# Moving the weights' scaling behind Z, and splitting the first sum rows, in a two-layer graph network on one core

## The chip, the cores and the metric

The kernel runs on one core of a Trainium2 chip. The metric is the device time of one execution in microseconds (us). Three runs of the kernel before took 913.83, 913.29 and 912.90 us; the median is 913.29.

## The reference, cut to what matters

x is 4096 x 256, adj a 4096 x 4096 matrix of zeros and ones. Two layers, each followed by a residual sum and a layer norm:

```python
# layer 0
deg = maximum((adj != 0).sum(-1), 1)
a_norm = rsqrt(deg) * (adj + I) * rsqrt(deg)     # one degree for rows and columns of a row: 1/deg
x = layernorm(x + relu((a_norm @ x + x) @ W0 + b0))
# layer 1
attn_a = sigmoid(concat(adj @ x, x) @ Wa.T + ba);  attn_b likewise with Wb, bb
h = x @ W_sa;  scores = (h @ a_left)[:, None] + (h @ a_right)[None, :]
e = where(adj != 0, exp(-leaky_relu(scores, 0.01)), 0)
x_a = e / (sum(e, 1) + 1e-5) @ h
x_b = adj @ (x @ W_gcnb) + b_gcnb
x = layernorm(x + sigmoid(attn_a * x_a + attn_b * x_b))
```

(`node_degree` comes in as a column, so both factors of a_norm belong to the row.)

## The kernel before, in words

The 4096 rows are 32 tiles of 128 (T=32). Everything is ordered by hand: each engine runs its own list of instructions in program order, and semaphores (`S[...]`) tie them together. There is no planner.

**Stage 1, Z.** Z = x @ W0. For each tile t, TensorE transposes x (`xt_step`, L1277), ScalarE copies the transpose out (`xt_copy`, L521), TensorE multiplies by W0 (`z_step`, L1288) into one of two banks (so `z_step(t)` waits until Z of t-2 is copied out), and ScalarE (first ten tiles) or VectorE copies Z out (`z_copy`, L526 and L810). Z is then split into a high fp16 part on ScalarE (`y_hi`, L533) and a low part on VectorE (`y_lo`, L837). In steady state the split of tile t-2 follows the copy of tile t; after the loop come the splits of tiles 30 and 31.

**The adjacency** arrives as 128 strips of 512 KB through a ring of six (RING). SP, the queue of the transfers, issues strip s after strip s-6 is cast (L334). Even strips are cast to one-byte codes by ScalarE (L513), odd ones by VectorE (L797). A quarter is 16 strips, and holds the codes for four row tiles; all codes of a quarter are also written to memory (L322), behind the issue of the strip six after its last.

**Stage 2, sums.** For each row tile n, `sum_rows` (L1305) adds adj rows times Z: two matmuls (high, low) for each of the 32 row blocks jb, into the bank of n. Rows 0 to 15 of tiles 0 to 3 are done during stage 1 (`pass0_rows`). Their rows 16 to 31 (OUTER=16) come after a wait for all 32 low parts (`ylo_ready`). When a tile is complete (`acc_done`), VectorE does `degree`, `residual`, `stats` (together `head(n)`, L950 to L978), GpSimd the power and the shift (L436, L439), ScalarE `normalize` (L549, gives `x1_ready`). TensorE transposes x1 (`t_step`, L1325; `t_step(0)` stands between tiles 2 and 3), ScalarE and VectorE split it (`x1t_copy` L558, `x1t_lo` L940), and `p_step` (L1340) multiplies it by the scaled weights `wps`. `proj_copies` on ScalarE and `h_lo`, `forms_lo` on VectorE turn this into operands of the later stages; `p_step(n)` also waits for `h_lo(n-1)`. From tile 4 on, a tile's t_step and p_step stand between quarters of its sum matmuls.

**The weights.** `weight_norm` (L859 to L861) ends with a maximum; GpSimd takes a power of it (L420); `weight_scale` (L866 to L876) waits for that (`alpha_pow`) and works out the scale and its relatives; `weight_parts` (L882, L884) write the high and low part of the weights, `wps`.

**Later stages** compute the adj products of layer 1 from seven products for each panel, and the attention with its exponentials, in a loop over 16 panels, with waits only on earlier work.

Of the kernel before, what the change touches and what calls it, by code (L numbers as in the profile page):

```python
# [17 lines left out]
T = N // P  # L18
# [4 lines left out]
PT = 4  # L23
# [5 lines left out]
ZACT = 10  # L29
ZLAG = 12  # L30
OUTER = 16
WTS = 13
WTS_AT = 8
WARM = 20
# [53 lines left out]
def build(nc, x, adj, W0, b0, Wsa, asa, Wg, bg, Wa, ba, Wb, bb, out):  # L88
# [121 lines left out]
    with ExitStack() as ctx:  # L210
        ps = ctx.enter_context(nc.psum_tensor("ps", [P, 8, 512], F32))
        block_sem = lambda name: ctx.enter_context(nc.semaphore(name))
        S = {}
# [60 lines left out]
        def h_place(n):  # L274

            return hst[:, n % 2] if n < T - 2 else fb[:, n]
# [129 lines left out]
        def _(pool):  # L406
# [14 lines left out]

            pool.wait_ge(S["wts_in"], 16 * (WTS - 1))

# [59 lines left out]
        def cast_waits(eng, s):  # L483

            qq = s // GS
            eng.wait_ge(strip_in[s % RING], 16 * (s // RING + 1))
            if qq >= SLOTS:
                eng.wait_ge(S["acc_done"], PT * (qq - SLOTS + 1))
                eng.wait_ge(codes_out[qq % SLOTS], 32 * (qq // SLOTS))

        def codes_of(s):
            return codes[:, s // GS % SLOTS, :, s % GS * SJ:(s % GS + 1) * SJ, :].rearrange("p h j i -> p j h i")
# [3 lines left out]
        def split_at(t):  # L496

            upto = lambda i: 0 if i < ZACT else min(i - 1, 2 * (i - ZACT) + 2)
            return range(upto(t - 1), T if t == T else upto(t))
# [285 lines left out]
        def _(dve):  # L785
# [7 lines left out]
            def cast(count):  # L793

                for s in [next(todo) for _ in range(count)]:
                    cast_waits(dve, s)
                    dve.tensor_scalar(codes_of(s), strip_of(s), float(EDGE - NONE), float(NONE),  # L797
                                      ALU.mult, ALU.add).then_inc(S["cast_dve"], 1)
# [8 lines left out]
            def z_copy(t):  # L807

                dve.wait_ge(S["z_done"], t + 1)
                dve.tensor_copy(zf[:, t, 0:D], ZP(t)).then_inc(S["zf_dve"], 1)  # L810
# [23 lines left out]
            def y_lo(t):  # L834

                dve.wait_ge(S["yhi_ready"], t + 1)
                dve.scalar_tensor_tensor(out=y[:, t, 1, 0:D], in0=zf[:, t, 0:D], scalar=sc[:, SX],  # L837
                                         in1=y[:, t, 0, 0:D], op0=ALU.mult, op1=ALU.subtract
                                         ).then_inc(S["ylo_ready"], 1)

            def weight_column(k, c):

                dve.wait_ge(S["wts_in"], 16 * (WTS - 1))
                st.then(dve.scalar_tensor_tensor(out=wsum[:, 0:D], in0=wp[:, k, WG:WC], scalar=1.0,
                                                 in1=asab[:, c * D:(c + 1) * D], op0=ALU.mult, op1=ALU.mult,
                                                 accum_out=wp[:, k, GC + 2 + c:GC + 3 + c]))
                st.sync()

            def weight_squares():

                flat = lambda a: a.rearrange("p k c -> p (k c)")
                st.then(dve.tensor_tensor(flat(wsq[:]), flat(wp[:]), flat(wp[:]), ALU.mult))
                st.sync()
                dve.tensor_tensor(wsq[:, 1, :], wsq[:, 0, :], wsq[:, 1, :], ALU.add).then_inc(S["wsq_ready"], 1)

            def weight_norm():

                dve.wait_ge(S["wsum_ready"], 1)
                st.then(dve.tensor_reduce(sc[:, TMP], wsum[:], AX, ALU.max))  # L859
                st.sync()  # L860
                dve.tensor_scalar(sc[:, WMX], sc[:, TMP], 1e-30, None, ALU.max).then_inc(S["wnorm_ready"], 1)  # L861

            def weight_scale():

                dve.wait_ge(S["alpha_pow"], 1)
                st.then(dve.tensor_scalar(sc[:, AL], sc[:, WN], F16_TOP / D ** 0.5, None, ALU.mult))  # L866
                st.sync()
                st.then(dve.reciprocal(sc[:, IAL], sc[:, AL]))
                st.sync()
                st.then(dve.tensor_scalar(sc[:, HINVA], sc[:, IAL], 1.0 / EDGE_VAL, None, ALU.mult))  # L870
                st.then(dve.tensor_scalar(bgb[:], bgb[:], sc[:, AL], 0.5 * EDGE_VAL, ALU.mult, ALU.mult))
                dve.memset(hst[:, :, :, HC:ROW], 0.0)
                st.then(dve.tensor_scalar(sc[:, EXS], sc[:, IAL], 1.0 / PROJ, None, ALU.mult))
                st.then(dve.tensor_scalar(sc[:, QSC], sc[:, IAL], -SLOPE / PROJ, None, ALU.mult))
                st.then(dve.tensor_scalar(sc[:, WS], sc[:, AL], D ** 0.5, None, ALU.mult))
                dve.tensor_scalar(sc[:, QB], sc[:, IAL], -SLOPE * F16_TOP, None, ALU.mult).then_inc(S["alpha_ready"], 1)  # L876

            def weight_parts(part):

                st.sync()  # L880
                if part == 0:
                    st.then(dve.tensor_scalar(wps[:, :, 0, :], wp[:], sc[:, WS], None, ALU.mult))  # L882
                else:
                    dve.scalar_tensor_tensor(out=wps[:, :, 1, :], in0=wp[:], scalar=sc[:, WS], in1=wps[:, :, 0, :],  # L884
                                             op0=ALU.mult, op1=ALU.subtract).then_inc(S["wps_ready"], 1)
# [7 lines left out]
            for t in range(ZACT, T):  # L893
                z_copy(t)
                for i in split_at(t):
                    y_lo(i)
                if 10 <= t < 26 and t % 2 == 0:
                    cast(1)
                if 18 <= t < 22:
                    weight_column((t - 18) // 2, t % 2)  # L900
                if t == 22:
                    weight_squares()
                if t == 26:
                    weight_norm()
                if t == 28:
                    weight_scale()
                if t in (29, 30):
                    weight_parts(t - 29)
            for t in split_at(T):
                y_lo(t)  # L910

# [10 lines left out]
            def h_lo(n):  # L922
                t, h = n, h_place(n)
                dve.wait_ge(S["hhi_ready"], n + 1)
                dve.scalar_tensor_tensor(out=h[:, 1, D:HC], in0=q[:, t:t + 1], scalar=KAPPA, in1=h[:, 0, D:HC],
                                         op0=ALU.mult, op1=ALU.subtract)
                dve.scalar_tensor_tensor(out=h[:, 1, 0:D], in0=BH, scalar=qa[:, t:t + 1],
                                         in1=h[:, 0, 0:D], op0=ALU.mult, op1=ALU.subtract
                                         ).then_inc(S["hlo_ready"], 1)
# [50 lines left out]
            def head(n):  # L980
                degree(n)
                residual(n)
                stats(n)

            cast(2)
            head(0)
            cast(2)
# [1 line left out]
            cast(2)  # L989
            x1t_lo(0)  # L990
            head(2)
            cast(2)
            head(3)
            h_lo(0)
            x1t_lo(1)
            cast(2)
            h_lo(1)
            forms_lo(0)
            x1t_lo(2)
# [264 lines left out]
        def _(pe):  # L1264
# [27 lines left out]
            def rows_cast(qq, jb):  # L1292

                strip_nr = qq * GS + jb // SJ
                mine = 0 if on_act(strip_nr) else 1
                pe.wait_ge(S[("cast_act", "cast_dve")[mine]], casts_until(strip_nr)[mine])

            def sum_rows(n, j0, j1):

                qq, h, e = n // PT, n % PT // 2, n % 2  # L1300
                for jb in range(j0, j1):
                    if jb % SJ == 0 and n % PT == 0:
                        rows_cast(qq, jb)
                    for part in range(2):
                        mm = pe.matmul(ACC(n), codes[:, qq % SLOTS, h, jb, e * P:(e + 1) * P].bitcast(F8),  # L1305
                                       y[:, jb, part, 0:YC], start=(jb == 0 and part == 0),
                                       stop=(jb == T - 1 and part == 1))
                if j1 == T:
                    mm.then_inc(S["acc_done"], 1)

            def pass0_rows(jb):

                pe.wait_ge(S["ylo_ready"], jb + 1)
                for n in range(PT):
                    sum_rows(n, jb, jb + 1)
# [29 lines left out]
            for t in range(T + 1):  # L1345
                if t < T:
                    xt_step(t)
                if t >= 1:
                    z_step(t - 1)
                if 0 <= t - 1 - ZLAG < OUTER:  # L1350
                    pass0_rows(t - 1 - ZLAG)
            pe.wait_ge(S["ylo_ready"], T)
            for n in range(PT):
                sum_rows(n, OUTER, T)
                if n == 2:
                    t_step(0)
# [184 lines left out]
```

## Time and profile before

| | us |
|---|---|
| median of three runs | 913.29 |
| the profiled execution | 912.75 |
| its span, first to last instruction | 911.0 |
| TensorE busy in the span | 863.7 (95%) |
| VectorE busy | 658.2 (72%) |
| ScalarE busy | 588.9 (65%) |
| GpSimd busy | 196.6 (22%) |
| mean granted TensorE clock | 0.984 |

The span runs from the first to the last instruction; the time of the execution is 1.75 us longer. Times in a trace count from the span's start. In the names of the views PE is TensorE's matmuls, PEld its weight loads, DVE VectorE, ACT ScalarE, POOL GpSimd and SP SyncE. "Idle before" is what the engine waited ahead of an instruction, and the arrow names what ended it.

### The profile page before, as it was taken

The page shows a single profiled execution, that of the slowest core. Times are in us where ns is not written, and L with a number is a line of the kernel's source. Part 1 is how long each engine was busy: PE and PEld are TensorE (multiplying, and loading weights), DVE is VectorE, ACT ScalarE, POOL GpSimd, SP SyncE. Part 2 cuts the span into 40 slices and gives each one's busy share as a digit, 9 for nine tenths or more (in the row PEclk, how much of TensorE's full clock was granted, in tenths as well). Part 3 has the DMA queues.
Part 4 walks back from the last instruction along what each step waited for, and adds up shares of the span by engine and source line. Part 5 has one row for each costly group of instructions (what it writes and reads, how often), then busy time and mean ns, then how long its engine had stood idle before and what let it go on. Part 6 is the DMA issues. An engine that isn't in the chain of part 4 may idle for free.

```text
span 911.0 us, 20479 instructions
## 1 busy us (share of the span) xinstructions
PE 863.7 (95%) x7573; PEld 756.6 (83%) x7573; DVE 658.2 (72%) x1145; ACT 588.9 (65%) x1245; POOL 196.6 (22%) x217
## 2 busy tenths in 40 slices
PE   8969999999999997978999999999999999999996
PEld 7757788888888885867888888888888888888885
DVE  5776565555556456868788788788788788788784
ACT  4744565655655437777686686686686686686662
POOL 1022343343343230100210210210210210210211
PEclk9999999999999998998999999999999999999998
DMA  9868899999999442101210211211211201201001
GB/s 317 307 220 322 316 344 351 372 313 329 375 309 354 150 151 85 54 13 42 76 53 25 75 33 42 75 30 45 75 30 45 75 26 49 75 27 48 24 24 36
DMA packets 67691, 130.02 MB, mean 143 GB/s; under 512 B 6545, under 2 KB 30129, under 8 KB 63153
## 3 DMA queue, kind: packets, MB, share of 16 engines
q1 hardware_dynamic: 58704, 120.87, 37.8%
q10 hardware_dynamic: 8928, 8.38, 2.8%
q8 instruction: 36, 0.59, 0.3%
q14 instruction: 23, 0.18, 0.1%
HBM read 99.87 MB, written 29.36 MB: 142 GB/s over the span
## 4 chain that ended last, share of the span: by engine, by line
DVE 30%; PE 29%; issue 18%; ACT 9%; POOL 7%; DMA 3%; SPq 1%; DVEq 1%; ACTq 1%; POOLq 0%
PE ps L1305 22%; DVE ec L1071 12%; ACT em L645 7%; DVE dd L934 6%; PE ps L1340 5%; POOL sc L459 4%; DVE em L1078 2%; PE ps L1393 2%; POOL sc L463 2%; DMA strip<-in_adj_dram 2%; DMA xs<-in_x_dram 1%; DVE sg L1152 1%; DVE sg L1143 1%; DVE sc L1156 1%; DVE s L1121 1%
## 5 line engine op out<-in xcount | busy, mean ns | idle before, releaser
L1439 PE MATMUL ps<-fb,em 128*128 128x257 f16 x3072 | 347.9, 273 | 1.4 <-issue 0.8
L1439 PEld LDWEIGHTS ps<-fb,em 128*128 128x128 f16 x3072 | 300.4, 98 | 39.2 <-issue 1.1
L1305 PE MATMUL ps<-y,codes 128*128 128x257 f16 x2048 | 240.8, 275 | 3.3 <-DVE y L837 3.3
L1305 PEld LDWEIGHTS ps<-y,codes 128*128 128x128 fp8e4 x2048 | 201.8, 99 | 31.7 <-DVE y L837 3.7
L636 ACT ACTIVATE ec<-slb,nsb 128x256 f32<-128x256 f32 x512 | 211.3, 496 | 0.2 <-DVE slb L1042 0.2
L1078 DVE SCALAR_TENSOR_TENSOR em<-ec,em 128x2048 f16<-128x2048 f32 x64 | 146.6, 2291 | 78.0 <-ACT em L645 77.7
L645 ACT ACTIVATE em<-ec 128x2048 f16<-128x2048 f32 x64 | 121.8, 1904 | 100.7 <-DVE ec L1071 100.7
L1071 DVE SCALAR_TENSOR_TENSOR ec<-ec,pan 128x2048 f32<-128x2048 f32 x64 | 146.1, 2283 | 0.0
L459 POOL TENSOR_TENSOR sc<-sc,sc 128x2 f32<-128x2 f32 x15 | 37.5, 2502 | 321.6 <-DVE sc L1161 321.6
L1393 PE MATMUL ps<-zz,dd 128*128 128x256 f16 x768 | 92.2, 278 | 7.4 <-DVE dd L934 7.4
L1393 PEld LDWEIGHTS ps<-zz,dd 128*128 128x128 fp8e4 x768 | 76.4, 100 | 18.1 <-issue 7.9
L513 ACT ACTIVATE codes<-strip 128x1024 uint8<-128x1024 f32 x64 | 66.6, 1047 | 10.5 <-DMA strip<-in_adj_dram 8.9
L1393 PE MATMUL ps<-fa,dd 128*128 128x260 f16 x512 | 60.9, 278 | 10.1 <-DVE m L1090 10.1
L1393 PEld LDWEIGHTS ps<-fa,dd 128*128 128x128 fp8e4 x512 | 49.7, 99 | 21.2 <-issue 14.1
L934 DVE SCALAR_TENSOR_TENSOR dd<-pan 128x512 uint32<-128x512 uint32 (+2 forms) x85 | 64.2, 815 | 0.0
L1393 PE MATMUL ps<-fa,pan 128*128 128x260 f16 x512 | 60.1, 275 | 3.0 <-DVE zz L920 3.0
L950 DVE TENSOR_SCALAR lnst<-ps 128x1 f32<-128x1 f32 x32 | 5.0, 157 | 80.0 <-PE ps L1305 80.0
L549 ACT ACTIVATE x<-x,lnst 128x256 f32<-128x256 f32 x32 | 19.2, 600 | 66.6 <-POOL lnst L439 66.6
L436 POOL TENSOR_TENSOR lnst<-lnst,sc 128x1 f32<-128x1 f32 x32 | 28.0, 876 | 144.1 <-DVE lnst L978 141.2
L1393 PEld LDWEIGHTS ps<-fa,pan 128*128 128x128 fp8e4 x512 | 50.0, 98 | 9.8 <-DVE zz L920 3.2
L453 POOL TENSOR_TENSOR w<-w,bgb 128x512 f32<-128x512 f32 x16 | 26.3, 1641 | 135.6 <-DVE w L1123 116.4
L797 DVE TENSOR_SCALAR codes<-strip 128x1024 uint8<-128x1024 f32 x64 | 42.4, 688 | 12.7 <-DMA strip<-in_adj_dram 12.7
(147 smaller groups left out, 804.4 us busy)
## 6 DMA issues: line engine op xcount, KB each, us to landing
strip<-in_adj_dram SPq DMA_DIRECT2D x128, 512.0 KB, 7.0
a_scratch<-codes SPq DMA_DIRECT2D x16, 1024.0 KB, 9.6
pan<-a_scratch SPq DMA_DIRECT2D x16, 1024.0 KB, 6.1
x_scratch<-x ACTq DMA_DIRECT2D x32, 128.0 KB, 5.4
x1r<-x_scratch SPq DMA_DIRECT2D x16, 256.0 KB, 2.8
h_scratch<-hst ACTq DMA_DIRECT2D x30, 136.0 KB, 5.2
out_dram<-ot SPq DMA_DIRECT2D x15, 256.0 KB, 2.2
fb<-h_scratch SPq DMA_DIRECT2D x3, 1088.0 KB, 8.6
```

The costliest lines, as they stand in the source:

```text
L459: pool.tensor_tensor(sc1[:, RS2], sc1[:, VE2], sc[:, MH2], ALU.pow).then_inc(S["yrstd_ready"], 1)
L513: act.activation(codes_of(s), strip_of(s), ACT.Copy, scale=float(EDGE - NONE), bias=float(NONE)).then_inc(S["cast_act"], 1)
L636: e_ = act.activation(ec[:, c % ER, jj, :], slb[:, slot, :], ACT.Exp, scale=-(1 - SLOPE), bias=nsb[:, jb:jb + 1])
L645: act.activation(em[:, c, 0], ec[:, c % ER], ACT.Copy, scale=MU / EDGE_VAL).then_inc(S["ehigh_ready"], 1)
L797: dve.tensor_scalar(codes_of(s), strip_of(s), float(EDGE - NONE), float(NONE), ALU.mult, ALU.add).then_inc(S["cast_dve"], 1)
L934: return dve.scalar_tensor_tensor(out=o, in0=b, scalar=0x7f7f7f7f, in1=a, op0=ALU.bitwise_and, op1=ALU.bitwise_xor)
L1071: dve.scalar_tensor_tensor(out=ec[:, c % ER], in0=ec[:, c % ER], scalar=1.0, in1=pan[:, slot, c * CH:(c + 1) * CH, :].bitcast(F8), op0=ALU ...
L1078: dve.scalar_tensor_tensor(out=em[:, c, 1], in0=ec[:, c % ER], scalar=MU / EDGE_VAL, in1=em[:, c, 0], op0=ALU.mult, op1=ALU.subtract).then ...
L1305: mm = pe.matmul(ACC(n), codes[:, qq % SLOTS, h, jb, e * P:(e + 1) * P].bitcast(F8), y[:, jb, part, 0:YC], start=(jb == 0 and part == 0), ...
L1340: mm = pe.matmul(b, x1t[:, n % 2, x_part, k * P:(k + 1) * P], wps[:, k, w_part, c0:c1], start=(k == 0 and x_part + w_part == 0), stop=(k = ...
L1393: mm = pe.matmul(ps[:, bank, 0:2 * c], a.bitcast(F8), g, start=(p == 0), stop=(p == NP - 1))
L1439: mm = pe.matmul(PH(2 * m + e)[:, 0:HC], em[:, c, e_part, i, e * P:(e + 1) * P], fb[:, jb, h_part, 0:HC], start=(jb == 0 and e_part + h_pa ...
```

## The change

Three edits. On VectorE, `weight_scale` and both `weight_parts` leave the loop over tiles 28 to 30 of stage 1 and stand after the last `y_lo`, ahead of the first casts of stage 2. On TensorE, rows 16 to 31 of tiles 0 and 1 are done in two parts: rows 16 to 27 of both after a wait for 28 low parts, then rows 28 to 31 of both after the wait for all 32. On VectorE again, in the hand-written start of stage 2, `head(3)` goes ahead of a cast of two, which becomes a cast of one behind it, and the next cast of two becomes one of three.

```diff
+LATE = 4
@@ VectorE, loop over t of stage 1
-                if t == 28:
-                    weight_scale()
-                if t in (29, 30):
-                    weight_parts(t - 29)
             for t in split_at(T):
                 y_lo(t)
@@ VectorE, start of stage 2
+            weight_scale()
+            for part in range(2):
+                weight_parts(part)
             cast(2)
             head(0)
             cast(2)
@@
             x1t_lo(0)
             head(2)
-            cast(2)
             head(3)
+            cast(1)
             h_lo(0)
             x1t_lo(1)
-            cast(2)
+            cast(3)
             h_lo(1)
@@ TensorE, behind the loop of stage 1
+
+            pe.wait_ge(S["ylo_ready"], T - LATE)
+            for n in range(2):
+                sum_rows(n, OUTER, T - LATE)
             pe.wait_ge(S["ylo_ready"], T)
-            for n in range(PT):
+            for n in range(2):
+                sum_rows(n, T - LATE, T)
+            for n in range(2, PT):
                 sum_rows(n, OUTER, T)
                 if n == 2:
                     t_step(0)
```

## Rows read from the trace of the kernel before

**Rows 1.** Table of stretches: length, busy us (instructions) by engine, TensorE's clock, DMA share, GB/s.

```profile
60.00:68.00 8.00, 1.47 (x6) 0.68 (x4) 5.46 (x19) 1.76 (x4) 2.02 (x3) 0.84 0.32 133
68.00:81.00 13.00, 12.53 (x97) 10.43 (x98) 8.13 (x23) 6.16 (x7) 2.65 (x4) 0.83 0.76 261
...
88.00:94.00 6.00, 3.81 (x31) 2.90 (x29) 4.72 (x14) 2.08 (x7) 2.04 (x3) 0.90 1.05 397
94.00:103.00 9.00, 8.43 (x67) 6.88 (x66) 3.18 (x9) 6.19 (x18) 1.65 (x3) 0.88 1.00 379
103.00:300.00 197.00, 197.00 (x1792) 175.28 (x1790) 114.22 (x337) 112.90 (x265) 74.80 (x105) 1.00 0.94 333
```

**Rows 2.** Chain of waits: start, length, what ended last there.

```profile
56.13 5.73 issue
61.85 0.60 POOL sc L420
...
81.02 6.95 DMA strip<-in_adj_dram
```

**Rows 3.** TensorE in order of time: start, length, line, operation, count, idle before.

```profile
57.17 1.03 PE L1288 MATMUL ps<-w,xt 128*128 128x256 f32 x4
...
59.34 1.03 PE L1288 MATMUL ps<-w,xt 128*128 128x256 f32 x4
...
64.04 1.10 PE L1288 MATMUL ps<-w,xt 128*128 128x256 f32 x4 [3.67 <-DVE zf L810]
68.47 12.60 PE L1305 MATMUL ps<-y,codes 128*128 128x257 f16 x96 [3.33 <-DVE y L837]
...
81.12 3.68 PE L1305 MATMUL ps<-y,codes 128*128 128x257 f16 x32
84.64 1.49 PE L1340 MATMUL ps<-wps,x1t 128*128 128x262 f16 x12
...
92.06 2.09 PE L1340 MATMUL ps<-wps,x1t 128*128 128x262 f16 x12 [2.19 <-DVE x1t L940]
93.95 3.04 PE L1305 MATMUL ps<-y,codes 128*128 128x257 f16 x16
...
99.53 1.50 PE L1340 MATMUL ps<-wps,x1t 128*128 128x262 f16 x12 [0.57 <-DVE x1t L940]
```

**Rows 4.** VectorE in order of time, 58 to 108 us.

```profile
58.24 0.43 DVE L810 COPY zf<-ps 128x256 f32<-128x256 f32 x1 [1.15 <-PE ps L1288]
58.58 0.48 DVE L837 SCALAR_TENSOR_TENSOR y<-zf,sc,y 128x256 f16<-128x256 f32 x1
62.48 0.15 DVE L866 TENSOR_SCALAR sc<-sc 128x1 f32<-128x1 f32 x1 [3.42 <-POOL sc L420]
...
64.21 0.75 DVE L882 TENSOR_SCALAR wps<-wp,sc 128x1036 f16<-128x1036 f32 x1
...
65.61 1.28 DVE L884 SCALAR_TENSOR_TENSOR wps<-wp,sc,wps 128x1036 f16<-128x1036 f32 x1
...
68.33 1.28 DVE L797 TENSOR_SCALAR codes<-strip 128x1024 uint8<-128x1024 f32 x2
74.06 0.16 DVE L950 TENSOR_SCALAR lnst<-ps 128x1 f32<-128x1 f32 x1 [4.45 <-PE ps L1305]
...
76.59 1.28 DVE L797 TENSOR_SCALAR codes<-strip 128x1024 uint8<-128x1024 f32 x2
...
88.00 0.69 DVE L797 TENSOR_SCALAR codes<-strip 128x1024 uint8<-128x1024 f32 x1 [2.25 <-DMA strip<-in_adj_dram]
...
106.43 1.28 DVE L797 TENSOR_SCALAR codes<-strip 128x1024 uint8<-128x1024 f32 x2
```

**Rows 5.** ScalarE in order of time, 66 to 80 us.

```profile
67.67 2.93 ACT L513 ACTIVATE codes<-strip 128x1024 uint8<-128x1024 f32 x3
...
78.31 0.60 ACT L549 ACTIVATE x<-x,lnst 128x256 f32<-128x256 f32 x1 [4.60 <-POOL lnst L439]
```

**Rows 6.** Transfers issued from 68.5 to 69.0: count, KB, us to landing (strip 22).

```profile
strip<-in_adj_dram SPq DMA_DIRECT2D x1, 512.0 KB, 3.9
```

## The prediction

> **What bounds the kernel now.** I first read the table of stretches [rows 1]. From 103 to 300 us TensorE is busy for all 197.00 us, at full clock; the DMA engines are at 0.94 there, and VectorE at 114 of 197. A microsecond gained on TensorE ahead of 103 us is therefore kept, if transfers and VectorE can follow; one gained elsewhere is worth nothing. Ahead of it lie 43 us with holes: 1.47 us busy of 8.00 in 60:68, then granted clocks of 0.83, 0.90 and 0.88 (a mix of TensorE's two levels, 1.2 and 2.4 GHz) with busy 12.53 of 13, 3.81 of 6, 8.43 of 9. The table above has TensorE busy 95% of the whole span, so the later stages pass an earlier start on too.
>
> TensorE in order of time [rows 3] names the holes: 3.67 us until the last Z step at 64.04 (waiting for a copy of Z on VectorE), 3.33 us until the first sum rows at 68.47 (for the last low part of Z), 2.19 us until p_step(1) at 92.06 and 0.57 until p_step(2) at 99.53 (both for x1t_lo). Cold clock: 96 sum matmuls at 68.47 took 12.60, where 32 at full clock take 3.52 from start to start (81.12 to 84.64), so 10.7 for 96: 1.9 lost. After the wait at 92.06, 12 projection matmuls took 2.09 against 1.49 at 84.64, and the 16 sum matmuls at 93.95 took 3.04 where half of the 3.68 at 81.12 is 1.84: another 1.8. All of it, 9.8 us of holes and 3.7 of cold clock, 13.5 us, is the most that edits here could give.
>
> The chain of waits [rows 2] says why: GpSimd's power (L420) started 5.73 us after its input was there, at 61.85. VectorE [rows 4] sat 3.42 us in weight_scale until 62.48, with the copies of Z 29 to 31 and the low parts 27 to 31 queued behind it. Those are what TensorE waited for in both of the first holes.
>
> **Edit 1: the weights' scale and parts go behind the last low part.** Z steps start 1.08 apart (57.17 to 59.34 are two). z_step(28), started at 57.17, released its copy at 58.24, 1.07 later. So the copy of Z 29 starts at 59.33 (VectorE is free from 58.58+0.48=59.06) and ends near 59.70. TensorE needs it for z_step(31), which then follows z_step(30) (59.34) at 60.2 in place of 64.04. TensorE is done with it at 61.1. VectorE: low 27 until 60.1, copy 30 from 60.4, low 28 until 61.15, copy 31 from 61.3, low 29, 30 and 31 behind it at 0.4 each: the last ends at 62.9. Nothing of this waits for GpSimd. Behind it come weight_scale (62.48 to 63.5: 1.0), the parts (0.75 and 1.28 [rows 4]) and two synchronisations of about 0.1 that the parts had other work in between for: until 66.0. Who waits for them: p_step(0) for the parts and proj_copies(0) for the scale, neither before 75.9. The power is done at 62.45, so it is just in time. The same instructions run, 3.1 us of them, no longer ahead of Z; they now stand ahead of the casts of strips 17 and 19 (1.28), which end at 67.2 instead of 69.6.
>
> **Edit 2: rows 16 to 27 of tiles 0 and 1, then their rows 28 to 31.** The new wait asks for low parts 0 to 27, done at 60.1, ahead of 61.1: it costs nothing. 48 matmuls at 3.52/32=0.11 are 5.3 us, until 66.4; all low parts are there at 62.9, so the second wait is free too. Without this edit the sums would begin at 62.9, 1.8 later. Its price: tile 0 ends after 56 matmuls, at 67.3, not after 32. VectorE isn't free before 67.2, so that is hidden.
> TensorE starts the sums at 61.1 instead of 68.47: **-7.4**. With no hole before it the clock stays at 2.4 GHz: **-1.9**. The bounds of the second are 0 and 1.9.
>
> **What is late next.** head(0) took from 74.06 to 76.6 [rows 4]; now 67.3 to 69.9. From there to x1 of tile 0 it took until 78.31+0.60 [rows 5], 2.3 behind the statistics: 72.15. TensorE ends tile 2 at 61.1+96*0.11=71.65 and waits for x1 in t_step(0): **+0.5**, a wait that before didn't have. Tile 3 then ends at 75.9.
> p_step(0) needs x1t_lo(0), which VectorE does behind head(1) and the casts of 21, 23, 25 and 27. Here the strips count. SP issues strip s only when s-6 is cast. Strip 22 goes out when ScalarE has cast 16: its casts began at 67.67 [rows 5], now at 62.3, so at 63.3; it lands 3.9 later [rows 6]. Strip 23 waits for cast 17, near 66.6, 24 to 26 follow, and 27 waits for cast 21, at 70.6. At 390 GB/s (397 in 88:94, 379 in 94:103 [rows 1]) a strip of 0.524 MB takes 1.35 us, so 23 lands at 70.5, 26 at 74.5 and 27 at 75.9. VectorE: casts 21 and 23 until 71.2, head(1) until 73.8, cast 25, wait, cast 27 until 76.6, x1t_lo(0) until 76.95. p_step(0) starts there, 7.7 earlier than 84.64, with a new wait of **+1.05** (bounds 0 and 3: strips under load landed after 3.9 to 6.95 us [rows 2, 6]).
>
> **Edit 3: head(3) ahead of the casts, one cast, then three.** Before, the cast of strip 31 waited 2.25 us for it, until 88.00 [rows 4], with head(3), h_lo(0) and x1t_lo(1), thus p_step(1), queued behind it. Now head(2) and head(3) run 76.95 to 82.2, cast 29 (long landed) until 82.8, h_lo(0) and x1t_lo(1) until 83.8. TensorE, free at 82.05, waits 1.8 in place of 2.19: **-0.4**; p_step(1) starts at 83.85, 8.2 earlier. In the old order cast 31 would land near 81.4 and head(3) end near 84.7, p_step(1) near 86: the edit is worth some 2 us. What it adds: strip 35 is issued only after cast 29, so at 82.8, lands at 87.5, and stands ahead of h_lo(1) in the cast of three. p_step(2) came 7.47 behind p_step(1) by a chain over ScalarE and GpSimd [rows 3]; 88.2 for the end of cast 35, then h_lo(1), three forms and x1t_lo(2) (2.2 us) give 90.4, the chain gives 90.7 to 91.3. So strip 35 is hidden, narrowly. Of the 1.8 us of cold clock here I take a fifth back (each wait is a little shorter than 2.19, but there are more of them): **-0.35**, bounds 0 and -1.8. ScalarE, too, has casts (28 and 30) ahead of proj_copies(0), and strip 30 lands near 80; hhi of tile 0 is then ready at 82.2, ahead of h_lo(0) at 82.8.
>
> Sum: -7.4-1.9+0.5+1.05-0.4-0.35 = **-8.5**. Profiled execution: 912.75 (span 911.0 and 1.75 around it) gives 904.25; the median of the runs, 913.29, lies 0.54 higher: **904.8**.
>
> **Can transfers follow?** From 67.6 to the landing of strip 39 the queues carry 17 strips (8.9 MB), 2.1 of codes and 0.5 of x and h: 11.5 MB, 29.5 us at 390 GB/s, so 97.1; VectorE ended cast 39 at 107.7 before (106.43+1.28) [rows 4], minus 8.5 is 99.2. It holds. Beyond, a tile needs 2.9 MB per 8.58 us, 336 GB/s, and recovers some more.
>
> **Rivals.**
> A. Strips set the pace. If 11.5 MB come at the 333 GB/s that 103:300 shows [rows 1] they need 34.5 us, until 102.1, and cast 39 is only some 5.2 earlier than before: 908.1. For it: DMA share is 1.05 in 88:94, and 0.94 for 200 us. Against: 397 GB/s was reached, and 333 is what a stage bound by TensorE asked for. A page of the Trainium skill, DMA: Bandwidth & Descriptors, section Where 436 GB/s comes from, says that transfers between HBM and SBUF are bound at about 358 GB/s for a core; by that the estimate would be 32.1 us for them, until 99.7, so cast 39 would be some 7.5 earlier than before and the gain about 7. The trace shows 397 over 6 us [rows 1], and the measurement decides; I give the page 0.05 of A's chance.
> B. A bigger gain: TensorE stays at full clock throughout and strip 27 lands before VectorE gets there: 8.5+1.35+1.05, near 902.3.
> C. No change: the gain is given back where TensorE was full, by VectorE waits for strips in 103:300, or at a later handover. It takes 8 us of new holes in a stage that had none; nothing in the rows shows them: 913.
> D. Slower: weight_scale now stands ahead of head(0), and the casts and their strips behind both. If the power's result came later than 62.9, head(0) and the ring of strips would be late by as much. From 71.4 on (8.5 later) all gain is gone; two more of the 5.73 us of [rows 2] would put it at 73.9, 11.0 later, and give 904.8+11.0=915.8. Against: its 5.73 us began at 56.13, before anything in the change, and GpSimd's order is untouched.
>
> **Chances.** Forecast (902.8 to 906.5) 0.62; A 0.18; B 0.10; C 0.05; D 0.05. The range leaves out C, D and the tails of A and B: 901.5 to 909. A measurement here tells about 0.2% (1.8 us) from no change. Faster by more 0.91, within it 0.05, slower 0.04.
>
> **What would show it.** Right: the first sum matmul near 61 with no hole before it, no clock below 1.00 in 60:80, the power at 61.85 as before, weight_scale without a wait, p_step(0) near 77, p_step(1) near 84, and p_step(2) near 91; 8.5 us less until the last matmul. Wrong: TensorE waits in tiles 3 to 6 for strips, holes behind 103 less the gain, or the power later.

## The result, and the profile after

The changed kernel took 907.35 us (median of four executions, 906.99 to 909.11) against 913.1 for the kernel before beside it. The ratio is 0.9943, 95% interval 0.9929 to 0.9957: 5.75 us faster by the medians, where 8.5 was forecast. Measured again with three relatives: 906.37 against 911.74, ratio 0.9941 (0.9923 to 0.9958). The profiled execution has a span of 905.5 us, 5.5 less than before.

TensorE of the changed kernel in order of time, from z_step(29) on (start, length, line, operation, count, idle before); it answers to [rows 3]:

```profile
57.47 1.03 PE L1288 MATMUL ps<-w,xt 128*128 128x256 f32 x4
...
58.55 1.89 PE L1288 MATMUL ps<-w,xt 128*128 128x256 f32 x8
60.28 10.72 PE L1305 MATMUL ps<-y,codes 128*128 128x257 f16 x96
71.95 0.44 PE L1325 MATMUL ps<-ident,x 128*128 128x128 f32 x2 [0.95 <-ACT x L550]
72.22 3.68 PE L1305 MATMUL ps<-y,codes 128*128 128x257 f16 x32
78.21 1.50 PE L1340 MATMUL ps<-wps,x1t 128*128 128x262 f16 x12 [2.31 <-DVE x1t L937]
...
85.16 1.50 PE L1340 MATMUL ps<-wps,x1t 128*128 128x262 f16 x12 [1.71 <-DVE x1t L937]
...
92.52 1.50 PE L1340 MATMUL ps<-wps,x1t 128*128 128x262 f16 x12 [2.12 <-DVE x1t L937]
93.86 1.92 PE L1305 MATMUL ps<-y,codes 128*128 128x257 f16 x16
```

The reader is to see that both holes ahead of the sums are gone, and that three new ones stand behind them: 0.95 ahead of t_step(0), 2.31 ahead of p_step(0), and 2.12 in place of 0.57 ahead of p_step(2). No matmul runs at the low clock (granted clock 1.00 from 56 to 103 us): 96 take 10.72, not 12.60.

In this trace all of stage 1 runs 0.8 us earlier than in the one of before (z_step(28) starts at 56.38, not 57.17 [rows 3]), although no edit touches it. I therefore count from the start of z_step(28). The sums start 3.90 behind it, before 11.30: -7.40, as forecast. p_step(1) starts 28.78 behind it (34.89 before), p_step(2) 36.14 (42.36 before): a lead of 6.2 us.

VectorE of the changed kernel, for [rows 4]:

```profile
60.82 1.97 DVE L838 SCALAR_TENSOR_TENSOR y<-zf,sc,y 128x256 f16<-128x256 f32 x3
62.71 0.14 DVE L867 TENSOR_SCALAR sc<-sc 128x1 f32<-128x1 f32 x1
...
66.95 0.15 DVE L947 TENSOR_SCALAR lnst<-ps 128x1 f32<-128x1 f32 x1
...
73.56 0.68 DVE L798 TENSOR_SCALAR codes<-strip 128x1024 uint8<-128x1024 f32 x1
77.13 0.69 DVE L798 TENSOR_SCALAR codes<-strip 128x1024 uint8<-128x1024 f32 x1 [2.88 <-DMA strip<-in_adj_dram]
77.74 0.42 DVE L937 SCALAR_TENSOR_TENSOR x1t<-ps,x1t 128x256 f16<-128x256 f32 x1
```

weight_scale (L867) waits for nothing. The cast at 77.13, of strip 27, waits 2.88 us, and x1t_lo(0), for which TensorE waits until 78.21, is queued behind it. ScalarE shows the same: its cast of strip 26 waited 2.93 us with x1t_copy(0) behind it, and its casts of 28 and 30 waited 0.90 and 1.93 with proj_copies(0) behind them. The chain of waits of the changed kernel has a strip as its longest piece between 56 and 100 us. It is strip 30, issued at 72.87 when strip 24 was cast:

```profile
71.90 0.95 ACT codes L514
72.87 8.58 DMA strip<-in_adj_dram
81.49 0.94 issue
```

So two engines met here. ScalarE cast strip 30 until 82.5 and had proj_copies(0), normalize(2) and x1t_copy(1) queued behind it; VectorE, held up by strip 27, ended head(3) and the cast of 29 at 83.8. x1t_lo(1), for which p_step(1) waited, then waited 0.20 for ScalarE. The two strips held p_step(1) about equally.

Strip 27 itself, the only one issued from 69.9 to 70.3 (last line below, of the transfers: count, KB, us to landing), took 6.9 us. The queues meanwhile were full: the table of stretches (last three numbers: TensorE's clock, DMA share, GB/s) has, of the changed kernel,

```profile
70.00:74.00 4.00, 3.05 (x29) 2.50 (x27) 3.51 (x11) 1.55 (x2) 2.13 (x4) 1.00 1.04 394
74.00:78.00 4.00, 1.91 (x18) 1.45 (x15) 1.12 (x3) 1.81 (x3) 1.60 (x3) 1.00 1.05 389
78.00:82.00 4.00, 3.79 (x35) 3.38 (x36) 3.69 (x14) 1.58 (x2) 1.15 (x3) 1.00 1.06 393
...
strip<-in_adj_dram SPq DMA_DIRECT2D x1, 512.0 KB, 6.9
```

From 103 to 200 us TensorE is busy for 97.00 of 97 in both kernels. At the handover to the layer-1 products (near 340 us) part of the lead goes, in this execution. The same 32 products, changed kernel, then the kernel before:

```profile
341.91 6.37 PE L1399 MATMUL ps<-fa,dd 128*128 128x260 f16 x32 [1.13 <-DVE m L1090]
```

```profile
349.01 5.26 PE L1393 MATMUL ps<-fa,dd 128*128 128x260 f16 x32 [0.57 <-DVE m L1090]
```

They start 7.10 earlier and end 6.0 earlier: at full clock such a group takes 3.71 (seen below), so both ran partly at the low clock, the changed kernel for longer. Another 0.55 goes near 386, where TensorE's wait under "issue" is 1.37 us, not 0.82. So 5.5 = 6.2 + 0.8 (stage 1) - 1.1 - 0.55, and 0.1 of rounding.

### The profile page after: what moved, and what is told of

It is laid out like the page before. It is cut to its first block, busy times and chain, and to the rows that moved or that the text cites. A ratio compares the mean times of both kernels' runs of the same rounds, so it can differ in the third digit from the quotient of the medians.

```text
span 905.5 us, 20480 instructions
## 1 busy us (share of the span) xinstructions
PE 860.3 (95%) x7573; PEld 755.2 (83%) x7573; DVE 660.7 (73%) x1145; ACT 588.8 (65%) x1245; POOL 196.3 (22%) x217
## 4 chain that ended last, share of the span: by engine, by line
PE 32%; DVE 28%; issue 17%; ACT 10%; POOL 7%; DMA 4%; SPq 1%; DVEq 1%; ACTq 1%; POOLq 0%
PE ps L1305 22%; DVE ec L1071 12%; ACT em L646 7%; DVE dd L931 6%; PE ps L1340 5%; POOL sc L460 4%; PE ps L1399 3%; DMA strip<-in_adj_dram 2%; POOL sc L464 2%; DVE em L1078 2%; DMA xs<-in_x_dram 1%; PE ps L1288 1%; DVE sg L1152 1%; DVE sg L1143 1%; DVE sc L1156 1%
## 5 line engine op out<-in xcount | busy, mean ns | idle before, releaser
L1305 PE MATMUL ps<-y,codes 128*128 128x257 f16 x2048 | 237.8, 273 | 0.0
L1399 PE MATMUL ps<-fa,dd 128*128 128x260 f16 x512 | 62.0, 281 | 10.4 <-DVE m L1090 10.2
```

What stands on the lines that cost most here:

```text
L1399: mm = pe.matmul(ps[:, bank, 0:2 * c], a.bitcast(F8), g, start=(p == 0), stop=(p == NP - 1))
```

## The experiments

The theory, S: once Z is clear of the power, casts that wait for strips and stand ahead of x1t_lo and proj_copies set p_step(0) to (2). Its rivals: K, the gain is that of the two holes and the chain over GpSimd and ScalarE sets the rest; R, later casts issue later strips and give it back. For each kernel the last column is 42.36 (the kernel before) less the start of p_step(2) behind that of z_step(28), in its one profile. The ratio is to the kernel before beside it; where two intervals overlap, the order of two kernels is not shown by them.

| kernel | median us (before) | ratio, 95% interval | lead at p_step(2) |
|---|---|---|---|
| edit 1 | 908.77 (912.13) | 0.9956, 0.9942 to 0.9970 | 2.9 |
| edits 1, 2 | 908.26 (912.13) | 0.9958, 0.9945 to 0.9971 | 4.5 |
| edit 2 | 912.22 (912.13) | 0.9990, 0.9980 to 1.0001 | -0.7 |
| edit 3 | 910.09 (912.13) | 0.9975, 0.9966 to 0.9984 | 2.2 |
| all three (changed kernel) | 906.37 (911.74) | 0.9941, 0.9923 to 0.9958 | 6.2 |
| changed, half strips | 902.53 (911.74) | 0.9889, 0.9870 to 0.9908 | 10.2 |
| changed, casts first | 904.36 (911.74) | 0.9917, 0.9899 to 0.9934 | 6.9 |
| changed, holes filled | 905.95 (911.74) | 0.9925, 0.9905 to 0.9945 | 6.4 |
| changed, copies first | 905.94 (912.50) | 0.9928, 0.9908 to 0.9949 | 7.1 |
| casts and copies first | 903.33 (912.50) | 0.9890, 0.9868 to 0.9911 | 8.5 |
| the same, holes filled | 902.60 (912.50) | 0.9892, 0.9870 to 0.9914 | 9.3 |
| before, one cast first | 910.24 (912.50) | 0.9977, 0.9965 to 0.9989 | 3.0 |

**Edit 1 alone.** (The edit is in the diff above.)

> The kernel before with the first edit alone: weights' scale and parts behind the last low part. Theory S (once Z is clear of the power, the strips set the pace through the casts that stand ahead of x1t_lo on VectorE): the sums start near 62, head(0) near 67, p_step(0) waits for the cast of strip 27 until about 78, p_step(1) until about 86.5 because strip 31 is cast ahead of head(3); gain 3 to 5 us. Rival K (strips play no part, the gain is that of the first two holes and their cold clock): gain 7 to 9 us.

3.4 us by the medians, as S has it. TensorE:

```profile
63.44 12.12 PE L1304 MATMUL ps<-y,codes 128*128 128x257 f16 x96 [2.66 <-DVE y L837]
...
79.13 1.49 PE L1339 MATMUL ps<-wps,x1t 128*128 128x262 f16 x12
...
88.02 2.77 PE L1339 MATMUL ps<-wps,x1t 128*128 128x262 f16 x12 [3.66 <-DVE x1t L936]
```

The wait that I expected ahead of p_step(0) was not there; p_step(1) waited 3.66, for x1t_lo(1) behind the cast of strip 31, which waited 2.30. Behind the hole of 2.66 ahead of the sums the low clock stayed (12.12), and behind that of 3.66 it came too (2.77 for 12 matmuls).

**Edits 1 and 2.**

> First and second edit, without the third (head(3) stays behind the casts of strips 29 and 31). Theory S: the sums start 1.8 us earlier than with the first edit alone, but head(0) starts where VectorE is free and x1t_lo(0) where strip 27 is cast, so the time is that of the first edit alone within 0.5 us. Rival K: another 1.8 us earlier than the first edit alone.

The same time as edit 1 alone (0.5 us by the medians, ratios 0.9958 and 0.9956), as S has it. The sums start 3.90 behind z_step(28), not 6.72, and TensorE has no low clock in them, but p_step(1) starts at 30.5 behind it where edit 1 alone has 31.3. Of the 2.8 us that edit 2 brings at the start of the sums, and 1.4 of clock in them, 0.8 is left at p_step(1).

**Edit 2 alone.**

> The second edit alone, with the weights' scale still in the loop: rows 16 to 27 of tiles 0 and 1 can start once low part 27 is there (near 65) instead of at 68.5. Theory S: head(0) moves from 74.1 to about 71.3 and with it the casts of strips 21 to 27; gain 2 to 3 us. Rival (the second edit has value only when Z is clear of the power): 0 within 0.5.

I missed here: no gain (ratio 0.9990), though the edit does move the sums. TensorE:

```profile
65.52 12.19 PE L1306 MATMUL ps<-y,codes 128*128 128x257 f16 x96
78.26 0.44 PE L1326 MATMUL ps<-ident,x 128*128 128x128 f32 x2 [0.55 <-ACT x L550]
78.53 3.68 PE L1306 MATMUL ps<-y,codes 128*128 128x257 f16 x32
83.92 1.50 PE L1341 MATMUL ps<-wps,x1t 128*128 128x262 f16 x12 [1.71 <-DVE x1t L941]
...
92.59 2.77 PE L1341 MATMUL ps<-wps,x1t 128*128 128x262 f16 x12 [3.43 <-DVE x1t L941]
```

The sums start 7.80 behind z_step(28) (11.30 before), p_step(1) 34.87 (34.89 before). The cast of strip 31, which stands ahead of head(3), starts 30.81 behind z_step(28), before 30.83: strips issued sooner did not land sooner. Strip 27 was issued 18.87 behind z_step(28), 1.3 sooner than before (20.13), and took 6.2 us; in the kernel before it was issued when only strip 26 was still to land, and took 3.7. It landed 1.2 later than before. So the number is the rival's. Its reason is not needed: the lost lead stands in the waits for strips, as S would have it, which I had not applied to this kernel. By what rule strip 27 landed late stays open: the queues moved 287 GB/s from 76 to 83 us, not 390.

**Edit 3 alone.**

> The third edit alone. Theory S: the cast of strip 31 (2.25 us of wait) no longer stands ahead of head(3); p_step(1) moves from 92.1 to near 90, and some of it goes back because strip 35 is issued later; gain 1 to 2 us. Rival (strip 35 gives it all back): 0 within 0.5; p_step(2) then stays near 99.5.

2.0 us, and p_step(1) started without a wait. Together the parts alone make 3.4 + 0 + 2.0 = 5.4 us, where all three bring 5.4 to 5.75.

**The changed kernel again.**

> The changed kernel again, to be compared with the next three on the same chip: 907.3, 5.5 to 6 us under the kernel before.

5.4 us under the kernel before by the medians, just short of the 5.5 to 6 expected. In its profile the low clock fell elsewhere: 12 projection matmuls of p_step(0) took 2.72 instead of 1.50, and the products at the handover 5.02 instead of 6.37; the span is 903.8. Two executions of one kernel differ by where the clock falls.

**Half strips.**

```diff
+HALF = (22, 40)
...
-                sp.dma_start(strip[:, s % RING], adj_view[:, g * SJ:(g + 1) * SJ, qq * 2 * PW:(qq + 1) * 2 * PW]
+                wide = PW if HALF[0] <= s < HALF[1] else 2 * PW
+                sp.dma_start(strip[:, s % RING, :, 0:wide],
+                             adj_view[:, g * SJ:(g + 1) * SJ, qq * 2 * PW:qq * 2 * PW + wide]
```

> The changed kernel with strips 22 to 39 loading only half of their columns (256 KB for 512 KB); everything else runs as before, on what lay in the rest of the buffers. Theory S (strips set the waits ahead of p_step(0), (1) and (2), 6.1 us in the changed kernel's profile): casts no longer wait between 70 and 90, those waits shrink to 1 to 2 us together, and the time falls by 2.5 to 5 us. Rival K (the waits come from the chain over GpSimd and ScalarE): it falls by less than 1 us.

This is the direct measurement: 3.84 us less than the changed kernel beside it, with no instruction of an engine changed; it leaves out half of the adjacency of 18 strips and computes something else. TensorE:

```profile
76.12 1.49 PE L1343 MATMUL ps<-wps,x1t 128*128 128x262 f16 x12
...
81.80 1.50 PE L1343 MATMUL ps<-wps,x1t 128*128 128x262 f16 x12 [0.44 <-DVE x1t L940]
...
88.75 1.50 PE L1343 MATMUL ps<-wps,x1t 128*128 128x262 f16 x12 [1.72 <-DVE x1t L940]
```

The wait at p_step(0) is gone, that at p_step(1) falls from 1.71 to 0.44. The third stays at 1.72: it is the chain from p_step(1) over ScalarE and GpSimd, 6.95 us from start to start here, 7.36 in the changed kernel, 7.47 before. The three waits came to 2.2 us, from 6.1. So S holds for the first two waits and K for the third. The lead at p_step(2) grew by 4.0 us, the time fell by 3.8.

**Casts first.**

```diff
+            cast(3)
             weight_scale()
             for part in range(2):
                 weight_parts(part)
-            cast(2)
             head(0)
-            cast(2)
+            cast(1)
             head(1)
```

> The changed kernel with the casts of strips 17, 19 and 21 (all landed by then) ahead of the weights' scale, and one cast for two behind head(0). The same instructions. Theory S: strips 23 to 27 are issued 3 to 6 us earlier, the queues are busy from 63 on, strip 27 no longer holds x1t_lo(0); head(0) is 0.6 later. Gain 1.5 to 3.5 us on the changed kernel. Rival K: 0.6 us slower.

2.0 us faster than the changed kernel by the medians, with the same instructions; the intervals overlap (0.9899 to 0.9934, 0.9923 to 0.9958), the single times hardly (at most 905.74, at least 905.64). The wait at p_step(0) fell from about 2.2 to 1.06; the cast of strip 27 still waited 2.28 us. Strip 27 was issued at 65.55, 4.6 us sooner than in the changed kernel, and took 10.7 us to land, not 6.9: its cast started 20.2 behind z_step(28) instead of 20.8. Most of the head start was lost. Why the queues moved only 213 GB/s from 63 to 67 us, and 393 from 69 to 73, stays open. Strip 26 was there in time (ScalarE waited 0.19 for it, not 2.93), and p_step(0) started 0.6 sooner behind z_step(28); the three casts made head(0) later, so that t_step(0) waited 1.61. At p_step(2) the profile shows 0.7 us of the 2.0. Its 32 products at the handover took 4.40, not 6.37 or 5.02 as in the two profiles of the changed kernel, so how much of the 2.0 is the strips' is not shown.

**Holes filled.** 24 transposes of the identity ahead of the last form, and 8 ahead of product M2, into a bank that nobody reads:

```diff
+FILL = (24, 8)
...
+            pe.wait_ge(S["g_ready"], T)
+            for _ in range(FILL[0]):
+                pe.transpose(ps[:, 4, 0:P], ident[:], ident[:])
             pe.wait_ge(S["forms_ready"], NP)
```

> The changed kernel with 24 and 8 idle transposes of the identity into a free bank in TensorE's holes at the handover to the layer-1 products (3.0 and 1.1 us, near 337 to 342). They compute nothing that is read. Theory W (1.1 us of the lead of 7.0 were lost there because TensorE's granted clock fell at another point of the holes): the first 32 products take 3.7 instead of 6.4 us, the time falls by 1.5 to 2.7 us. Rival: the loss was later waits, and it stays within 0.5.

```profile
339.48 2.78 PE L1429 MATMUL ps<-ident 128*128 128x128 f32 x24
342.68 0.40 PE L1400 MATMUL ps<-fa,pan 128*128 128x260 f16 x2 [0.42 <-DVE zz L918]
342.91 0.60 PE L1400 MATMUL ps<-zz,dd 128*128 128x256 f16 x4
343.35 1.04 PE L1438 MATMUL ps<-ident 128*128 128x128 f32 x8
344.68 3.71 PE L1400 MATMUL ps<-fa,dd 128*128 128x260 f16 x32 [0.30 <-DVE m L1091]
```

The profile does what W said: 3.71 us for the 32 products. The time did not show it: 0.4 us by the medians, far inside the intervals, and what the rival forecast. This profile had 1.7 us of low clock at p_step(2) that the changed kernel's first one had not. W is shown for that place; its worth in the median is not.

**Copies first.** On VectorE x1t_lo(0) and head(2) ahead of the cast of strip 27, on ScalarE proj_copies(0), normalize(2), x1t_copy(1) ahead of the cast of 30:

```diff
             head(1)
-            cast(2)
+            cast(1)
             x1t_lo(0)
             head(2)
+            cast(1)
             head(3)
```

> The changed kernel, with work that needs no strip moved ahead of two casts that wait for one: on VectorE x1t_lo(0) and head(2) ahead of the cast of strip 27, on ScalarE proj_copies(0) to x1t_copy(1) ahead of the cast of strip 30. Theory S (what costs is not that the strips are late but that the casts waiting for them stand ahead of x1t_lo and proj_copies): the wait of 2.1 to 2.3 us ahead of p_step(0) falls under 0.5, p_step(1) starts about 2 us earlier than in the changed kernel; gain 1.5 to 3 us on it. Rival K (the chain over GpSimd and ScalarE sets p_step(1) and (2) anyway): within 0.5. Rival R (later casts issue later strips, and the queues give it back): slower by up to 1.

0.4 us by the medians, 1.2 by the ratios (0.9928 and 0.9941), whose intervals overlap: inconclusive, and less than the 1.5 to 3 expected. p_step(0) waited 1.50, not under 0.5: x1t_copy(0) still stood behind ScalarE's cast of strip 26, which waited 2.72. I had moved casts 27 and 30 and left 26.

**Both orders.**

> The same order of copies and casts on top of the kernel with the casts of 17, 19 and 21 ahead of the weights' scale (904.4 us). Theory S: p_step(0) without a wait, p_step(1) about 2 us earlier than there; 902.5 to 903.5. Rivals as above: 904 to 905.

The time is in the range of S, 1.0 us under casts first by the medians, but the intervals overlap; clear of the changed kernel's it is. With strip 26 landed in time by the first order, the second works, as TensorE shows:

```profile
78.21 1.49 PE L1342 MATMUL ps<-wps,x1t 128*128 128x262 f16 x12
...
84.07 1.50 PE L1342 MATMUL ps<-wps,x1t 128*128 128x262 f16 x12 [0.63 <-DVE x1t L938]
...
92.14 2.49 PE L1342 MATMUL ps<-wps,x1t 128*128 128x262 f16 x12 [2.84 <-DVE x1t L938]
```

p_step(0) has no wait, p_step(1) 0.63, and R did not happen as a whole. A part of it did: VectorE's casts of 33 and 35 waited 1.81 and 2.34, both ahead of h_lo(1), and p_step(2) waited 2.84, not 2.12, with the low clock behind. This profile is of the slowest of the six executions (907.14 us).

**Both orders, holes filled.**

> The kernel before this one with the 24 and 8 idle transposes at the handover to the layer-1 products. Theory W (cold clock there costs what the profiles show: 32 products in 4.4 to 6.4 us, 3.7 when filled): another 1 to 2 us, 901 to 902.5. Rival: nothing, within 0.5.

902.60 against 903.33, the same within the intervals: the rival again, not the 1 to 2 us of W. It is, with the kernel before it, the best that computes everything: 9.9 us under the kernel before beside it, and clear of the changed kernel's interval.

**The kernel before, one cast first.** Only the cast of strip 21 moves, into time in which VectorE was idle:

```diff
-            cast(2)
+            cast(3)
             head(0)
-            cast(2)
+            cast(1)
```

> The kernel before, with only the cast of strip 21 moved ahead of head(0), where VectorE had 4.45 us of idle time. Z, the weights and the sums are as before. Theory S: strip 27 is issued at 71 instead of 77.3, the strips behind it come earlier, the cast of strip 31 no longer waits 2.25 us ahead of head(3), p_step(1) comes 1 to 2 us earlier; gain 1 to 2 us. Rival K: 0 within 0.5.

2.3 us by the medians (ratio 0.9977); strip 27 was issued at 70.55, the cast of strip 31 waited 1.11, not 2.25, and p_step(1) came 32.5 behind z_step(28) in place of 34.89. So even with the power's hole in place, a cast ahead of a wait was worth as much as edit 3.

## Why the prediction was right, and where its size was off

The time lay inside the range (901.5 to 909) and the gain had the forecast's sign, but it lay outside the narrower band of the forecast (902.8 to 906.5), and nearer to rival A's 908.1 than to 904.8; the gain was 5.75 of 8.5 us. The mechanism was right; two of its terms were too small. By the steps:

- **Edit 1 and 2, start of the sums, -7.4.** Measured -7.40 against z_step(28). The power (L421) came at 59.93 in the changed kernel, never later than 62.2 in any kernel here; rival D did not occur.
- **Clock, -1.9.** Measured -1.88 (10.72 for 12.60). It needs both edits: edit 1 alone left 12.12.
- **t_step(0), +0.5.** Measured from start to start, 11.67 for 96 matmuls of 10.56: +1.1. The three last low parts took 1.97, not 1.2, while GpSimd added its bias (60.51 to 62.1), and head(0) started 10.57 behind z_step(28), not 10.13. GpSimd's shift took 0.59 as well, where 0.26 is usual.
- **p_step(0), +1.05: the step that failed.** It waited 2.31, 2.5 from start to start. I let strips land one after the other at 1.35 us each, so that strip 27 landed 5.3 behind its issue, 18.7 behind z_step(28). It took 6.9 and landed at 20.7. Of these 2.0 us, 0.7 is that the cast of strip 17 ended later than I had it, behind the slow low parts, and so strip 23 came later. The other 1.3 is one gap: strips 23, 24, 25 and then 26, 27, 28, 29 did land 1.33 to 1.36 apart, but between 25 (73.10) and 26 (75.75) lay 2.65. The queues were not slower (389 to 394 GB/s). From the issue of strip 23 at 66.46 they had moved 296 GB/s for 6.64 us when 25 landed, 320 for 9.29 when 26 did:

```profile
66.46:73.10 6.64, 5.69 (x52) 4.85 (x50) 6.01 (x17) 2.53 (x3) 2.22 (x3) 1.00 0.83 296
66.46:75.75 9.29, 8.34 (x76) 7.10 (x73) 7.09 (x20) 2.53 (x3) 4.09 (x6) 1.00 0.88 320
```

  That is some 3.7 strips' worth for the three that had landed, then 5.7 for four. So strips issued after 26 had a share of the rate ahead of its landing, which my sum gave them none of. What sets the share is not shown. The bounds I named there (0 and 3, from landings after 3.9 to 6.95) held the truth; the trace of before even had landings after 7.4 and 8.7 us (strips 26 and 33). ScalarE's cast of strip 26 waited for the same reason, and x1t_copy(0) behind it; that edge I did not cost at all.
- **p_step(1), -0.4.** Measured -0.48. The time came out, the path only in part: strip 30, put near 80 (22.8 behind z_step(28)), landed 25.1 behind it, and was no longer hidden; ScalarE's chain behind it held x1t_lo(1) 0.20 longer than VectorE's.
- **Low clock behind p_step(1), -0.35.** It vanished there in this trace: -1.66; and p_step(2) waited 1.55 more from start to start. Together -0.1. The wait follows from the chain that I used for p_step(2), but not from the sum, where it stands in no term.
- Sum at p_step(2): forecast -8.5, measured -6.2. t_step(0), 0.6 over, and p_step(0), 1.4 over, are 2.0 of the 2.3; only the second is a wait for strips.
- **Later stages pass it on.** They did in 103 to 335 us. At the handover 1.1 us went by the clock in one trace and 0.2 came back in the other.

Rival A gave nearly the right time (908.1) by a wrong means: it had the queues slower, at 333 GB/s. They ran at 390. The cast of strip 39 did end at 102.58, 5.1 earlier than before and close to A's 5.2, behind a wait of 1.79 for its strip; but no wait of TensorE followed from it (97.00 us busy of 97 behind 103). What decided was which work was queued behind a cast that waited, ahead of 93 us. The estimate from the Trainium skill's 358 GB/s (DMA: Bandwidth & Descriptors, Where 436 GB/s comes from) falls with it: three stretches of 4 us had 389 to 394.

**Edit 3** was put at some 2 us; alone it brought 2.0, and without it the kernel is 1.9 slower by the medians, 1.5 by the ratios, with intervals that overlap. **Edit 2** was put at 1.8 on top of edit 1; it brought 0.5 by the medians without edit 3, which is not clear of zero.

## What to carry to other kernels

When a hole is closed, list for each engine the waiting instructions that stand ahead of the one the next stage needs, and move work that waits for nothing in front of them. Do not work out a transfer's landing from the sizes ahead of it and the rate alone: here that gave 5.3 us, measured were 6.9. Take the landing times of like transfers under a like load from the trace, and price the edge by the longest of them as well. Two profiles of one kernel can differ by 1 to 2 us at a place of low clock; compare starts against an instruction that no edit touches.

## What was not expected of the hardware

- Strip 22, with no other in flight, landed after 3.7 to 4.0 us (3.95 in the changed kernel); strip 27, with strips ahead of it and behind it, after 6.9 us there and 10.7 with casts first. Issuing them sooner moved the landing of the awaited one by little (edit 2 alone: by nothing at strip 31).
- A low part (L838), 0.47 us elsewhere, took 0.96 beside GpSimd's additions in the changed kernel, and 2.40 beside its all-reduce in the kernel before. The Trainium skill (SBUF — State Buffer, section SBUF: two separate sides) says that VectorE and GpSimd share a port pair as an exclusive lock, held for a whole instruction, and that a VectorE operation with two inputs in SBUF takes part in it against a GpSimd operation that reads SBUF. The trace agrees that such an operation is held up; not that it is held to the other's end: the low part beside the all-reduce ended at 52.47, the all-reduce at 53.29 (ends on GpSimd are rough).
- The 32 products at the handover, behind a wait of 3.0 us and a short one, took 4.39 to 6.60 us in the twelve profiles without the filling, 3.71 in both filled ones. The same kernel had 6.37 and 5.02, so the share of low clock (1.2 GHz) behind the same holes differs between executions. The three longest (6.37 to 6.60) came behind a short wait of 0.85 to 1.24 us, the other nine (4.39 to 5.62) behind one of 0.49 to 0.70; what decides it is not shown.
